# The mixer's chain: products two steps ahead, GpSimd's work reordered, and unread products on TensorE

## The chip, the cores and the metric

The kernel runs on one core of a Trainium2 chip, as one launch. The metric is device time in microseconds (us). Engines are TensorE (PE; PEld is its weight load), VectorE (DVE), ScalarE (ACT), GpSimd (POOL) and SyncE (SP, which only issues transfers here). Each engine runs its own instructions in order and waits on semaphores for the others. Numbers of lines are those of the kernel before.

## The reference, cut to what matters

The whole program is a small vision tower: an embedding, a recurrent mixer, a mixture of experts, a spiking attention, an attention block and MLPs. The change is in the mixer (`_L0_attn_ref`). With batch 4, 513 tokens, 6 heads of 64 channels and 8 states per head it computes

```
z  = s * (z - d * a * xs + d * bu)        # bu = B[t] (8) outer u[t] (64), per head
xs = xs + d * z
y[t] = C[t] . xs                          # sum over the 8 states
out = ((y + D_skip * u) * silu(gate)) @ w_out
```

one token after the other. s, d and a are numbers per token and head.

## The kernel before

The recurrence is linear, so the kernel cuts each sequence into chunks of L = 57 tokens: 9 chunks by 4 sequences make 36 steps. `mixer_responses` has computed on DVE how each lane answers (G_s, end_trans). `mixer_bc` (L1087) prepares B and C for all steps, and `mixer_chain` (L1224) walks the 36 steps, chunk by chunk with the four sequences in turn, so that a step needs the state of the step four before it. fp32 values are used in two fp16 parts, a high one and the rest ("low").

Each step n of the chain has these parts; the names in brackets are used in the text.

- POOL masks C by head: 6 copies of C side by side, each with the rows of one head, for C's high part (L1282, cbh) and for its low part (L1287, cbl). It also makes the matrix that carries the state on (L1294, [transition], for the first 32 steps), and multiplies the finished result of an earlier step with the gate (L1275, [gate]).
- PE turns u into tokens by channels (L1327, [turn], 3 fp32 transposes), carries the old state (L1355) and reads it out (L1356), both from the fifth step on ([old]), forms C times B for all heads (L1336 and L1338, [CB], 342 columns each), adds the end of chunk to the state (L1365, [send], 6 products, first 32 steps), and multiplies u with the mixing matrix (L1374, [y], 12 products of 57 columns).
- ACT rounds u to fp16 (L1312, [u high]), rounds the mixing matrix into two places (L1316, [wh], two copies), and scales u by D_skip (L1318, [D], three pieces).
- DVE takes u's rest (L1386, [u low]), multiplies CB with G_s into the mixing matrix (L1391, [matrix]), masks the new state (L1411, [state]), takes the matrix's rest (L1398, [low]; it reads two operands in SBUF), and adds D_skip times u to y (L1421, [yd]).

The order is written out by hand in each engine's block, with buffers for two steps. ACT's order is u high(n), wh(n), D(n), then u high(n+1). DVE's is u low(n+1), matrix(n+1), state(n), low(n+1), yd(n). PE's is turn(n+1), old(n), CB(n+1), send(n), y(n). POOL's is cbh(n), cbl(n), transition(n), gate(n-2).

In `mixer_bc`, PE transposes C scaled, B and C in 15 groups, ACT copies them out of PSUM as fp16 (B once, C twice, since C's high part stands in two row ranges under the low part of B), and DVE subtracts for the low parts (`low_part`). After B's low parts DVE computes the end-of-chunk matrices (L1218), ACT rounds them (L1167, L1168) and POOL subtracts (L1155), which ends the block. The halves lie in `c.xT`, a tile that is used again later and whose row DH holds ones.

`spin` (L128) issues 256-column fp16 products of ones that nobody reads; the kernel before uses it in other stages, not here. A block ends when all engines have ended theirs; `to_tokens` (L796) then multiplies by w_out.

Of the kernel before, what the change touches and what calls it, by code (L numbers as in the profile page):

```python
# [7 lines left out]
ALU = mybir.AluOpType  # L8
# [21 lines left out]
L = 57  # L30
# [96 lines left out]

def spin(c, pe, n):  # L128

    ones = c.ones[:, :].bitcast(F16)
    for _ in range(n):
        pe.matmul(c.bank[7][:, 0:256], ones[:, 0:128], ones, start=True, stop=True)  # L134

# [599 lines left out]
def mixer(c):  # L735

    with ExitStack() as ctx:
# [20 lines left out]
        half.ch = place[0][0:112, NT:2 * NT]  # L758
        half.cl = place[1][0:48, 0:NT]
        half.wh = c.sb(ctx, "B_end_high", [128, NBC * 96], F16)  # L760
# [326 lines left out]
def mixer_bc(c, ctx, raw, gs, ab, zx, acT, half):  # L1087
# [30 lines left out]
    with nc.Block() as block:  # L1118
# [24 lines left out]
        @block.gpsimd  # L1143
        def _(pool):

            pool.memset(acT[0:96].rearrange("p b s k t -> p (b s k t)"), 0.0).then_inc(zeroed, 1)  # L1146
            pool.wait_ge(zeroed, 1)
            pool.memset(half.b[32:64, :], 0.0).then_inc(zeroed, 1)
            pool.memset(half.ch[32:64, :], 0.0).then_inc(zeroed, 1)
            pool.memset(half.wh[32:64, :], 0.0).then_inc(zeroed, 1)  # L1150
            for r in (32, 64):
                pool.memset(half.wl[r:r + r, :], 0.0).then_inc(zeroed, 1)
            pool.wait_ge(zeroed, 6)
            pool.wait_ge(bwh, 2)
            pool.tensor_tensor(half.wl[0:L, :], bwf, half.wh[0:L, :], ALU.subtract).then_inc(bwl, 1)  # L1155

        @block.scalar
        def _(act):
            act.activation(bcn[0:L].rearrange("p a b c -> p (a b c)"), raw[:, :], ACT.Square).then_inc(squares, 1)
            act.wait_ge(sm, 1)  # L1160
            act.activation(sr[0:L, :], ss[0:L, :], ACT.Sqrt).then_inc(rt, 1)
            act.wait_ge(zeroed, 4)
            for n in range(len(jobs)):
# [6 lines left out]
                if kind == 0:  # L1170
                    act.copy(half.b[0:48, cols], ps[0:48]).then_inc(high, 1)
                elif kind == 1:
                    act.copy(half.ch[0:48, cols], ps[0:48]).then_inc(high, 1)
                    act.copy(half.ch[64:112, cols], ps[0:48]).then_inc(high, 1)
                else:
                    for b, ch, m, at in started(n):
                        for g in range(3):
                            rows = slice(32 * g, 32 * g + 32)
                            act.copy(acT[rows, b, ch - 1:ch - 1 + m, g, :],
                                     ps[rows, at * L:(at + m) * L].rearrange("p (a t) -> p a t", a=m)).then_inc(acd, 1)  # L1180

        @block.vector
        def _(dve):
# [19 lines left out]
            def low_part(n):  # L1203
                kind, cols, ps = job(n)
                dve.wait_ge(high, n - 4 if kind == 0 else 5 + 2 * (n - 9))
                if kind == 0:
                    dst, hi = half.b[64:112, cols], half.b[0:48, cols]
                else:
                    dst, hi = half.cl[:, cols], half.ch[0:48, cols]
                dve.tensor_tensor(dst, ps[0:48], hi, ALU.subtract).then_inc(low, 1)  # L1210
# [13 lines left out]
def mixer_chain(c, ctx, sg, vT, gs, acT, half, de, dsk, wo, wo_in):  # L1224

    nc = c.nc
    LOW = 64  # L1230
    K = LOW + L
    cbh = c.sb(ctx, "C_by_head_high", [112, 2, SH, L], F16)
    cbl = c.sb(ctx, "C_by_head_low", [112, 2, SH, L], F16)
    mask = c.sb(ctx, "head_mask", [112, SH], F16)
# [10 lines left out]
     s_done, s_ready) = map(c.sem, names)  # L1245
    skipped, padded = (c.sem(q) for q in ("Du_ready", "chain_padded"))
    N = NBC
    steps = [(ch, b, b * NC1 + ch) for ch in range(NC1) for b in range(BATCH)]
    last = N - BATCH
    with nc.Block() as block:  # L1250
# [5 lines left out]
        def _(pool):  # L1256

            for r in (32, 64):
                pool.memset(wl[r:r + r, :, :, :], 0.0).then_inc(padded, 1)
                pool.memset(cbl[r:(64, 112)[r // 64], :, :, :], 0.0).then_inc(padded, 1)  # L1260
            pool.wait_ge(padded, 4)
            pool.memset(u[32:64, :, :], 0.0).then_inc(init, 1)
# [8 lines left out]
            def gate(n):  # L1271
# [4 lines left out]
                pool.wait_ge(gated, n + 1)  # L1276

            for n, (ch, b, bc_) in enumerate(steps):
                cols = slice(bc_ * L, (bc_ + 1) * L)
                if n >= 2:  # L1280
                    pool.wait_ge(cb_done, n - 1)
                pool.tensor_tensor(cbh[:, n % 2, :, :], half.ch[:, cols].unsqueeze(1).broadcast_to((112, SH, L)),  # L1282
                                   mask[:, :].unsqueeze(2).broadcast_to((112, SH, L)), ALU.mult).then_inc(cbd_ready, 1)
                if n:
                    pool.wait_ge(cbd_ready, 2 * n)
                pool.wait_ge(cbd_ready, 2 * n + 1)
                pool.tensor_tensor(cbl[0:48, n % 2, :, :], half.cl[:, cols].unsqueeze(1).broadcast_to((48, SH, L)),  # L1287
                                   mask[0:48, :].unsqueeze(2).broadcast_to((48, SH, L)), ALU.mult
                                   ).then_inc(cbd_ready, 1)
                pool.wait_ge(cbd_ready, 2 * n + 2)  # L1290
                if n < last:
                    if n >= 2:
                        pool.wait_ge(s_done, n - 1)
                    pool.tensor_tensor(tm[:, n % 2, :].rearrange("p (h z m) -> p h z m", z=2, m=ST),  # L1294
                                       c.const("same", 96).rearrange("p (h z m) -> p h z m", z=2, m=ST),
                                       de[:, :, bc_].unsqueeze(1).unsqueeze(3).broadcast_to((96, SH, 2, ST)), ALU.mult
                                       ).then_inc(tm_ready, 1)
                    pool.wait_ge(tm_ready, n + 1)
                if n >= 2:
                    gate(n - 2)  # L1300
            for n in (N - 2, N - 1):
                gate(n)

        @block.scalar
        def _(act):
            act.wait_ge(init, 2)
            for n in range(N):
                act.wait_ge(u_t, n + 1)
# [3 lines left out]
                act.copy(u[0:L, n % 2, :], c.bank[n % 2][0:L, 0:DIN]).then_inc(u_high, 1)  # L1312
                cols = slice(steps[n][2] * L, (steps[n][2] + 1) * L)
                act.wait_ge(wt_ready, n + 1)
                for r in (0, LOW):
                    act.copy(wh[r:r + L, n % 2, :, :], wt[:, n % 2, :, :]).then_inc(wt_high, 1)  # L1316
                for k in range(3):
                    act.activation(vT[:, k, cols], vT[:, k, cols], ACT.Copy, scale=dsk[:, k:k + 1]).then_inc(skipped, 1)  # L1318

        @block.tensor  # L1320
        def _(pe):
# [8 lines left out]
            def c_times_b(n):  # L1330
                cols = slice(steps[n][2] * L, (steps[n][2] + 1) * L)
                pe.wait_ge(cbd_ready, 2 * n + 2)
                if n >= 2:
                    pe.wait_ge(wt_ready, n - 1)
                ps = c.bank[2 + n % 2][0:L, 0:SH * L]
                pe.matmul(ps, half.b[:, cols], cbh[:, n % 2, :, :].rearrange("p a b -> p (a b)"),  # L1336
                          start=True, stop=False)
                pe.matmul(ps, half.b[:, cols], cbl[:, n % 2, :, :].rearrange("p a b -> p (a b)"),  # L1338
                          start=False, stop=True).then_inc(cb_done, 1)

            turn(0)
            pe.wait_ge(padded, 4)
            c_times_b(0)
            for n, (ch, b, bc_) in enumerate(steps):
                old = state[:, b, (ch - 1) % 2, :]
                ybank, send = c.bank[4 + n % 2], c.bank[6 + n % 2][0:96, 0:2 * SP]
                if n + 1 < N:
                    turn(n + 1)
                if n >= 2:
                    pe.wait_ge(y_used, n - 1)  # L1350
                if ch:
                    pe.wait_ge(s_ready, n - BATCH + 1)
                    if n < last:
# [3 lines left out]
                              start=True, stop=False, skip_group_check=True)  # L1357
                if n + 1 < N:
                    c_times_b(n + 1)
                pe.wait_ge(u_low, n + 1)  # L1360
# [19 lines left out]
        def _(dve):  # L1380
            def prepare(n):
                ch, b, bc_ = steps[n]
                dve.wait_ge(u_high, n + 1)
                if n >= 2:
                    dve.wait_ge(y_done, n - 1)
                dve.tensor_tensor(u[LOW:LOW + L, n % 2, :], c.bank[n % 2][0:L, 0:DIN], u[0:L, n % 2, :], ALU.subtract  # L1386
                                  ).then_inc(u_low, 1)
                dve.wait_ge(cb_done, n + 1)
                if n >= 2:
# [10 lines left out]

            dve.wait_ge(padded, 4)
            prepare(0)
            low_part(0)
            for n, (ch, b, bc_) in enumerate(steps):
                if n + 1 < N:
                    prepare(n + 1)
                if n < last:
# [11 lines left out]
                if n >= 2:  # L1419
                    dve.wait_ge(gated, n - 1)  # L1420
                dve.tensor_tensor(yd[:, n % 2, :, :], c.bank[4 + n % 2][:, 0:3 * L].rearrange("p (k t) -> p k t", k=3),  # L1421
                                  vT[:, :, bc_ * L:(bc_ + 1) * L], ALU.add).then_inc(y_used, 1)


# [1712 lines left out]
```

## Time and profile before

| | us |
|---|---|
| median of 3 runs | 1843.28 (1840.26 to 1844.48) |
| profiled execution | 1847.83, its span 1846.0 |
| PE, DVE, ACT, POOL busy | 1513.2, 1306.5, 1053.0, 411.4 |
| chain's block, from its first turn to its last gate | 527.3 to 654.5 |

PE's busy time counts matmuls as pipelined work with modelled ends, so that a full 20 of 20 us need not be full speed. PEclk is the share of TensorE's 2.4 GHz that was granted: 1.00 is 2.4 GHz and 0.50 is 1.2 GHz. The page's 40 slices, 46 us each, show it by stage:

```profile
PEclk9999997688555588987999756999598889999898
```

Slices 11 to 14 of them (from 461 us to 646 us) are the scan's end, `mixer_bc` and the chain. An x behind a row is the count of instructions. "Idle before, releaser" in brackets is the time in which the engine stood still before the first of them, and what ended it.

### The profile page before, as it was taken

The page shows a single profiled execution, that of the slowest core. Times are in us where ns is not written, and L with a number is a line of the kernel's source. Part 1 is how long each engine was busy: PE and PEld are TensorE (multiplying, and loading weights), DVE is VectorE, ACT ScalarE, POOL GpSimd, SP SyncE. Part 2 cuts the span into 40 slices and gives each one's busy share as a digit, 9 for nine tenths or more (in the row PEclk, how much of TensorE's full clock was granted, in tenths as well). Part 3 has the DMA queues.
Part 4 walks back from the last instruction along what each step waited for, and adds up shares of the span by engine and source line. Part 5 has one row for each costly group of instructions (what it writes and reads, how often), then busy time and mean ns, then how long its engine had stood idle before and what let it go on. Part 6 is the DMA issues. An engine that isn't in the chain of part 4 may idle for free. (4 is left out here: it accounts for less than half of the span.)

```text
span 1846.0 us, 36517 instructions
## 1 busy us (share of the span) xinstructions
PE 1513.2 (82%) x14190; PEld 1135.7 (62%) x14190; DVE 1306.5 (71%) x2831; ACT 1053.0 (57%) x1872; POOL 411.4 (22%) x428
## 2 busy tenths in 40 slices
PE   5898995877349987899999854998198899999795
PEld 5888985776326675764444544888086554446474
DVE  5988895489646655837999375887365469995666
ACT  6988994433356616444998423665100548896455
POOL 0000000000357711036980013665000320000100
PEclk9999997688555588987999756999598889999898
DMA  5120001000000010002540092121200000000101
GB/s 138 27 65 23 14 2 48 1 4 1 1 7 1 1 33 1 14 1 104 180 131 2 1 271 66 56 62 50 73 1 5 9 2 2 2 2 2 33 1 35
DMA packets 52725, 67.96 MB, mean 37 GB/s; under 512 B 11511, under 2 KB 41465, under 8 KB 52554
## 3 DMA queue, kind: packets, MB, share of 16 engines
q1 hardware_dynamic: 46586, 50.74, 9.0%
q0 software_dynamic: 3840, 9.18, 1.7%
q10 hardware_dynamic: 2128, 5.71, 1.2%
q8 instruction: 114, 1.87, 0.4%
q14 instruction: 57, 0.47, 0.1%
HBM read 46.97 MB, written 18.65 MB: 36 GB/s over the span
## 5 line engine op out<-in xcount | busy, mean ns | idle before, releaser
L2007 DVE TENSOR_REDUCE att_max<-banks 104x1 f32<-104x512 f32 (+1 forms) x480 | 295.9, 682 | 9.7 <-PE banks L1921 5.7
L2042 ACT ACTIVATE att_p<-banks 104x514 f32<-104x514 f32 (+1 forms) x480 | 262.3, 600 | 33.3 <-PE banks L1966 22.6
L339 PE MATMUL banks<-tok_wT,feature_halves 128*128 128x192 f16 x2592 | 229.5, 249 | 22.9 <-DVE feature_halves L365 11.8
L339 PEld LDWEIGHTS banks<-tok_wT,feature_halves 128*128 128x128 f16 x2592 | 217.4, 99 | 31.8 <-DVE feature_halves L365 17.5
L1982 PE MATMUL banks<-att_p,att_v 104*32 104x257 f32 (+1 forms) x1920 | 159.8, 405 | 0.9 <-ACT att_p L2042 0.3
L1966 PE MATMUL banks<-att_q,att_kT 64*104 64x257 f16 (+1 forms) x960 | 155.9, 304 | 2.9 <-ACT att_p L2042 2.5
L1921 PE MATMUL banks<-att_kT,att_q 64*104 64x512 f16 (+1 forms) x480 | 126.3, 424 | 4.9 <-DVE att_max L2007 2.1
L365 DVE TENSOR_TENSOR feature_halves<-features,feature_halves 128x2048 f16<-128x2048 f32 x54 | 123.4, 2285 | 6.1 <-ACT feature_halves L462 6.1
L1966 PEld LDWEIGHTS banks<-att_q,att_kT 64*104 64x104 f16 (+1 forms) x960 | 61.8, 123 | 107.0 <-ACT att_p L2042 80.2
L1146 POOL MEMSET C_start_apart<- 96x5472 f32 x1 | 4.7, 4658 | 476.0 <-POOLq L972 476.0
L462 ACT CAST feature_halves<-features 128x2048 f16<-128x2048 f32 x54 | 102.2, 1893 | 10.8 <-PE banks L339 10.0
L134 PE MATMUL banks<-ones 128*128 128x256 f16 x450 | 59.9, 302 | 56.3 <-PEq L113 27.3
L134 PEld LDWEIGHTS banks<-ones 128*128 128x128 f16 x450 | 48.1, 108 | 67.9 <-issue 53.7
L2761 ACT COPY slot_xT<-banks 128x512 f16<-128x512 f16 x40 | 23.4, 586 | 93.4 <-PE banks L2711 93.4
L2740 PE MATMUL banks<-expert_w,slot_hidden_halves 128*128 128x192 f16 x720 | 65.8, 246 | 12.1 <-DVE slot_hidden_halves L2809 12.1
L2724 PE MATMUL banks<-slot_xT,expert_w 128*128 128x128 f16 x1200 | 75.7, 223 | 0.0
L1819 DVE TENSOR_TENSOR att_qkv_parts<-banks,att_qkv_parts 104x192 f16<-104x192 f32 (+1 forms) x80 | 25.0, 354 | 70.7 <-ACT att_qkv_parts L1799 70.7
L354 DVE SCALAR_TENSOR_TENSOR angle_rest<-raw_T,freq,turns 128x1024 f32<-128x1024 f32 x54 | 69.0, 1278 | 6.2 <-ACT turns L244 5.7
L2699 POOL DMA_INDIRECT expert_out<-slot_y,slot_goes x40 | 61.4, 1536 | 49.1 <-DMA expert_out<-slot_y,slot_goes 38.2
L1758 PE MATMUL banks<-att_qkv_w,xT 96*104 96x384 f32 (+3 forms) x160 | 66.7, 543 | 6.7 <-POOL att_qkv_parts L1734 4.5
L2724 PEld LDWEIGHTS banks<-slot_xT,expert_w 128*128 128x128 f16 x1200 | 72.0, 100 | 0.0
L1921 PEld LDWEIGHTS banks<-att_kT,att_q 64*104 64x104 f16 (+1 forms) x480 | 51.9, 126 | 31.3 <-DVE att_max L2007 19.2
(463 smaller groups left out, 3532.6 us busy)
## 6 DMA issues: line engine op xcount, KB each, us to landing
expert_w_in<-in_L_ffn_w_dram SPq DMA_DIRECT2D x16, 576.0 KB, 4.5
expert_w_halves<-expert_w_halves SPq DMA_DIRECT2D x32, 288.0 KB, 2.5
tok_w<-in_L_tok_W_dram ACTq DMA_DIRECT2D x4, 1152.0 KB, 7.3
expert_w2s<-expert_w_halves SPq DMA_DIRECT2D x1, 4608.0 KB
expert_y<-expert_out SPq DMA_DIRECT2D x6, 513.0 KB
expert_w1s<-expert_w_halves SPq DMA_DIRECT2D x2, 1536.0 KB
raw<-in_x_dram SPq DMA_DIRECT2D x2, 1152.0 KB, 5.7
expert_w1s<-expert_w_halves SPq DMA_DIRECT2D x3, 768.0 KB
```

The source lines that it names most:

```text
L134: pe.matmul(c.bank[7][:, 0:256], ones[:, 0:128], ones, start=True, stop=True)
L339: ins = pe.matmul(c.bank[t // 2][:, (t % 2) * D:(t % 2 + 1) * D], fh[:, s, q, z, t * 128:(t + 1) * 128], wT[:, y, k, 6 * q + wf, :], start ...
L354: own.did(dve.scalar_tensor_tensor(fr[:, n % 2, :], rT[:, k, hf * HALF:(hf + 1) * HALF], freq_col(k, f), fm[:, n % 2, :], ALU.mult, ALU.su ...
L365: dve.tensor_tensor(fh[:, s, :, 1, :], feat[:, s, :, :], fh[:, s, :, 0, :], ALU.subtract).then_inc(flow, 1)
L462: act.copy(fh[:, s, :, 0, :], feat[:, s, :, :]).then_inc(fhigh, 1)
L1758: ins = pe.matmul(c.bank[n % 2][0:m, 0:2 * D], c.xT[0:r, o, at:at + m], w[0:r, o, 0:2 * D], start=(o == 0), stop=(o == 1))
L1921: pe.matmul(bank_of(("s", n))[0:qn, 0:KEYS], q2[r, 2 * j + gi, b * T + q0:b * T + q0 + qn], kT[r, 2 * j + gi, b * T:b * T + KEYS], start=T ...
L1966: pe.matmul(c.pair[2 + n % 2][0:kn, 512 * e:512 * e + HALF], kT[r, 2 * j + gi, b * T + k0:b * T + k0 + kn], q2[r, 2 * j + gi, b * T + STAR ...
L1982: ins = pe.matmul(acc[32 * hh:32 * hh + 32, 0:HALF], v[0:kn, b, k, h, :], p[0:kn, (n + hh // 2) % 4, hh % 2, :], start=(k == 0), stop=(k = ...
L2007: dve.reduce_max(mx[0:qn, n // NS % 2, 2 * gi + e, k:k + 1], bank_of(unit)[0:qn, 0:KEYS], X).then_inc(maxed, 1)
L2042: act.activation(p[0:kn, n % 4, :, :], c.pair[2 + n % 2][0:kn, :].rearrange("p (e q) -> p e q", e=2)[:, :, 0:HALF], ACT.Exp, scale=scale). ...
L2724: ins = pe.matmul(ps, ws[:, s, at:at + 128], xt[:, s, b, :], start=(k == 0), stop=(k == len(TERMS) - 1))
```

## The change

- CB needs one masked tile: C's high and low parts stand under each other (rows 0 to 47 and 64 to 111) and B in two tiles, its high part in both row ranges and its low part over zeros. So B is copied twice in `mixer_bc` and C once, POOL masks once per step (cbd, as many columns and rows as cbh), and two more memsets clear B's second tile.
- That tile covers the row of ones in `c.xT`; POOL writes it again behind the last gate (1 x 1026 fp32).
- PE's turn, CB and with it DVE's matrix run two steps ahead, not one. DVE's order is then u low(n+1), state(n), low(n+1), yd(n), matrix(n+2).
- POOL's order is cbd(n), gate(n-3), transition(n-1).
- PE issues 36 unread products between turn(1) and the first CB, and 3 before each CB, into the bank that CB then overwrites.

```diff
-def spin(c, pe, n):
+def spin(c, pe, n, bank=7):
-        pe.matmul(c.bank[7][:, 0:256], ones[:, 0:128], ones, start=True, stop=True)
+        pe.matmul(c.bank[bank][:, 0:256], ones[:, 0:128], ones, start=True, stop=True)
...
-        half.cl = place[1][0:48, 0:NT]
+        half.bl = place[1][0:112, 0:NT]
...
+            pool.memset(half.bl[32:64, :], 0.0).then_inc(zeroed, 1)
             pool.memset(half.wh[32:64, :], 0.0).then_inc(zeroed, 1)
+            pool.memset(half.bl[64:112, :], 0.0).then_inc(zeroed, 1)
-            pool.wait_ge(zeroed, 6)
+            pool.wait_ge(zeroed, 8)
...
-            act.wait_ge(zeroed, 4)
+            act.wait_ge(zeroed, 5)
...
                 if kind == 0:
                     act.copy(half.b[0:48, cols], ps[0:48]).then_inc(high, 1)
+                    act.copy(half.b[64:112, cols], ps[0:48]).then_inc(high, 1)
                 elif kind == 1:
                     act.copy(half.ch[0:48, cols], ps[0:48]).then_inc(high, 1)
-                    act.copy(half.ch[64:112, cols], ps[0:48]).then_inc(high, 1)
...
-                dve.wait_ge(high, n - 4 if kind == 0 else 5 + 2 * (n - 9))
+                dve.wait_ge(high, 2 * (n - 4) if kind == 0 else n + 1)
                 if kind == 0:
-                    dst, hi = half.b[64:112, cols], half.b[0:48, cols]
+                    dst, hi = half.bl[0:48, cols], half.b[0:48, cols]
                 else:
-                    dst, hi = half.cl[:, cols], half.ch[0:48, cols]
+                    dst, hi = half.ch[64:112, cols], half.ch[0:48, cols]
                 dve.tensor_tensor(dst, ps[0:48], hi, ALU.subtract).then_inc(low, 1)
...
-    cbh = c.sb(ctx, "C_by_head_high", [112, 2, SH, L], F16)
-    cbl = c.sb(ctx, "C_by_head_low", [112, 2, SH, L], F16)
+    cbd = c.sb(ctx, "C_by_head", [112, 2, SH, L], F16)
...
             for r in (32, 64):
                 pool.memset(wl[r:r + r, :, :, :], 0.0).then_inc(padded, 1)
-                pool.memset(cbl[r:(64, 112)[r // 64], :, :, :], 0.0).then_inc(padded, 1)
-            pool.wait_ge(padded, 4)
+            pool.wait_ge(padded, 2)
...
+            def transition(n):
+                bc_ = steps[n][2]
+                if n >= 2:
+                    pool.wait_ge(s_done, n - 1)
+                pool.tensor_tensor(tm[:, n % 2, :].rearrange("p (h z m) -> p h z m", z=2, m=ST),
+                                   c.const("same", 96).rearrange("p (h z m) -> p h z m", z=2, m=ST),
+                                   de[:, :, bc_].unsqueeze(1).unsqueeze(3).broadcast_to((96, SH, 2, ST)), ALU.mult
+                                   ).then_inc(tm_ready, 1)
+                pool.wait_ge(tm_ready, n + 1)
             for n, (ch, b, bc_) in enumerate(steps):
                 cols = slice(bc_ * L, (bc_ + 1) * L)
                 if n >= 2:
                     pool.wait_ge(cb_done, n - 1)
-                pool.tensor_tensor(cbh[:, n % 2, :, :], half.ch[:, cols].unsqueeze(1).broadcast_to((112, SH, L)),
+                pool.tensor_tensor(cbd[:, n % 2, :, :], half.ch[:, cols].unsqueeze(1).broadcast_to((112, SH, L)),
                                    mask[:, :].unsqueeze(2).broadcast_to((112, SH, L)), ALU.mult).then_inc(cbd_ready, 1)
-                if n:
-                    pool.wait_ge(cbd_ready, 2 * n)
-                pool.wait_ge(cbd_ready, 2 * n + 1)
-                pool.tensor_tensor(cbl[0:48, n % 2, :, :], half.cl[:, cols].unsqueeze(1).broadcast_to((48, SH, L)),
-                                   mask[0:48, :].unsqueeze(2).broadcast_to((48, SH, L)), ALU.mult
-                                   ).then_inc(cbd_ready, 1)
-                pool.wait_ge(cbd_ready, 2 * n + 2)
...
-                if n >= 2:
-                    gate(n - 2)
-            for n in (N - 2, N - 1):
+                pool.wait_ge(cbd_ready, n + 1)
+                if n >= 3:
+                    gate(n - 3)
+                if 1 <= n <= last:
+                    transition(n - 1)
+            for n in (N - 3, N - 2, N - 1):
                 gate(n)
+            pool.wait_ge(cb_done, N)
+            pool.memset(c.xT[DH:DH + 1, 1, 0:NT // 2], 1.0).then_inc(ones_row, 1)
...
-            act.wait_ge(init, 2)
-            for n in range(N):
+            def highs(n):
                 act.wait_ge(u_t, n + 1)
                 if n >= 2:
                     act.wait_ge(y_done, n - 1)
                     act.wait_ge(s_done, min(n - 1, last))
                 act.copy(u[0:L, n % 2, :], c.bank[n % 2][0:L, 0:DIN]).then_inc(u_high, 1)
-                cols = slice(steps[n][2] * L, (steps[n][2] + 1) * L)
                 act.wait_ge(wt_ready, n + 1)
                 for r in (0, LOW):
                     act.copy(wh[r:r + L, n % 2, :, :], wt[:, n % 2, :, :]).then_inc(wt_high, 1)
+            act.wait_ge(init, 2)
+            for n in range(N):
+                highs(n)
+                cols = slice(steps[n][2] * L, (steps[n][2] + 1) * L)
                 for k in range(3):
                     act.activation(vT[:, k, cols], vT[:, k, cols], ACT.Copy, scale=dsk[:, k:k + 1]).then_inc(skipped, 1)
...
             def c_times_b(n):
                 cols = slice(steps[n][2] * L, (steps[n][2] + 1) * L)
-                pe.wait_ge(cbd_ready, 2 * n + 2)
+                pe.wait_ge(cbd_ready, n + 1)
                 if n >= 2:
                     pe.wait_ge(wt_ready, n - 1)
                 ps = c.bank[2 + n % 2][0:L, 0:SH * L]
-                pe.matmul(ps, half.b[:, cols], cbh[:, n % 2, :, :].rearrange("p a b -> p (a b)"),
+                spin(c, pe, 3, 2 + n % 2)
+                pe.matmul(ps, half.b[:, cols], cbd[:, n % 2, :, :].rearrange("p a b -> p (a b)"),
                           start=True, stop=False)
-                pe.matmul(ps, half.b[:, cols], cbl[:, n % 2, :, :].rearrange("p a b -> p (a b)"),
+                pe.matmul(ps, half.bl[:, cols], cbd[:, n % 2, :, :].rearrange("p a b -> p (a b)"),
                           start=False, stop=True).then_inc(cb_done, 1)
 
             turn(0)
-            pe.wait_ge(padded, 4)
+            turn(1)
+            spin(c, pe, 36, 4)
+            pe.wait_ge(padded, 2)
             c_times_b(0)
+            c_times_b(1)
             for n, (ch, b, bc_) in enumerate(steps):
                 old = state[:, b, (ch - 1) % 2, :]
                 ybank, send = c.bank[4 + n % 2], c.bank[6 + n % 2][0:96, 0:2 * SP]
-                if n + 1 < N:
-                    turn(n + 1)
+                if n + 2 < N:
+                    turn(n + 2)
                 if n >= 2:
                     pe.wait_ge(y_used, n - 1)
                 if ch:
@@ -1355,8 +1364,8 @@
                         pe.matmul(send, tm[:, n % 2, :], old, start=True, stop=False, skip_group_check=True)
                     pe.matmul(ybank[:, 0:3 * L], old, acT[0:96, b, ch - 1, :, :].rearrange("p k t -> p (k t)"),
                               start=True, stop=False, skip_group_check=True)
-                if n + 1 < N:
-                    c_times_b(n + 1)
+                if n + 2 < N:
+                    c_times_b(n + 2)
...
-            def prepare(n):
-                ch, b, bc_ = steps[n]
+            def u_low_part(n):
                 dve.wait_ge(u_high, n + 1)
                 if n >= 2:
                     dve.wait_ge(y_done, n - 1)
                 dve.tensor_tensor(u[LOW:LOW + L, n % 2, :], c.bank[n % 2][0:L, 0:DIN], u[0:L, n % 2, :], ALU.subtract
                                   ).then_inc(u_low, 1)
+            def matrix(n):
+                ch, b, bc_ = steps[n]
...
-            dve.wait_ge(padded, 4)
-            prepare(0)
+            dve.wait_ge(padded, 2)
+            matrix(0)
+            u_low_part(0)
+            matrix(1)
             low_part(0)
             for n, (ch, b, bc_) in enumerate(steps):
                 if n + 1 < N:
-                    prepare(n + 1)
+                    u_low_part(n + 1)
...
+                if n + 2 < N:
+                    matrix(n + 2)
```

## Rows read from the trace of the kernel before

**Rows 1.** Windows of the chain: PE, PEld, DVE, ACT, POOL busy (x), then PEclk

```profile
560.00:593.25 33.25, 33.25 (x271) 21.54 (x270) 20.79 (x51) 21.21 (x62) 25.48 (x40) 0.50 0.01 2
643.00:653.00 10.00, 6.80 (x54) 4.20 (x56) 5.46 (x13) 6.39 (x19) 4.57 (x7) 0.50 0.00 0
```

**Rows 2.** Instructions on the mixing matrix: ns min/median/max, first and last start

```profile
L1391 DVE TENSOR_TENSOR mix_matrix<-banks,G_s x36: 505/506/507, 534.4 to 650.8; 57x342 f32<-57x342 f32 x36
L1398 DVE TENSOR_TENSOR mix_matrix_low<-mix_matrix,mix_matrix_high x36: 506/508/706, 535.9 to 652.3; 57x342 f16<-57x342 f32 x36
```

**Rows 3.** Timeline of one step, DVE and ACT: start, us

```profile
587.59 0.51 DVE L1391 TENSOR_TENSOR mix_matrix<-banks,G_s 57x342 f32<-57x342 f32 x1
588.13 0.98 ACT L1316 CAST mix_matrix_high<-mix_matrix 57x342 f16<-57x342 f32 x2 [1.16 <-DVE mix_matrix L1391]
589.13 0.81 ACT L1318 ACTIVATE u_T<-u_T,D_skip 128x57 f32<-128x57 f32 x3
589.14 0.62 DVE L1398 TENSOR_TENSOR mix_matrix_low<-mix_matrix,mix_matrix_high 57x342 f16<-57x342 f32 x1 [0.84 <-ACT mix_matrix_high L1316]
589.69 0.32 DVE L1421 TENSOR_TENSOR y_plus_Du<-banks,u_T 128x171 f32<-128x171 f32 x1
589.85 0.45 ACT L1312 CAST u_halves<-banks 57x384 f16<-57x384 f32 x1
590.34 0.55 DVE L1386 TENSOR_TENSOR u_halves<-banks,u_halves 57x384 f16<-57x384 f32 x1 [0.33 <-ACT u_halves L1312]
```

**Rows 4.** Timeline of the same step, PE

```profile
587.46 0.89 PE L1327 MATMUL banks<-consts,u_T 128*57 128x128 f32 x3
588.15 0.63 PE L1355 MATMUL banks<-xT,transition 96*96 96x128 f32 x2
589.28 0.49 PE L1336 MATMUL banks<-C_by_head_high,xT 112*57 112x342 f16 x1
589.98 0.30 PE L1365 MATMUL banks<-u_halves,B_end_high 121*32 121x128 f16 x3
590.77 0.89 PE L1327 MATMUL banks<-consts,u_T 128*57 128x128 f32 x3
```

**Rows 5.** Timeline of the same step, POOL

```profile
589.05 0.35 POOL L1294 TENSOR_TENSOR transition<-consts,end_trans 96x96 f32<-96x96 f32 x1
590.15 0.51 POOL L1275 TENSOR_TENSOR gate_silu<-y_plus_Du,gate_silu 128x171 f32<-128x171 f32 x1 [0.76 <-PE banks L1338]
590.75 0.76 POOL L1282 TENSOR_TENSOR C_by_head_high<-xT,head_mask 112x342 f16<-112x342 f16 x1
```

**Rows 6.** Timeline of a step in which POOL's mask and DVE's low part overlap

```profile
598.59 0.75 POOL L1287 TENSOR_TENSOR C_by_head_low<-xT,head_mask 48x342 f16<-48x342 f16 x1
599.12 0.59 DVE L1398 TENSOR_TENSOR mix_matrix_low<-mix_matrix,mix_matrix_high 57x342 f16<-57x342 f32 x1 [0.84 <-ACT mix_matrix_high L1316]
```

**Rows 7.** Windows of unread products (first two) and of a looser stage, to PEclk

```profile
318.00:320.00 2.00, 2.00 (x12) 1.42 (x10) 0.50 0.42 35
324.00:326.00 2.00, 2.00 (x21) 1.79 (x20) 1.00 0.04 8
688.00:692.00 4.00, 4.00 (x26) 2.31 (x24) 2.98 (x10) 2.54 (x3) 1.15 (x1) 1.00 0.01 2
```

**Rows 8.** Timeline of the chain's start and its end

```profile
527.30 0.86 PE L1327 MATMUL banks<-consts,u_T 128*57 128x128 f32 x3 [17.79 <-PEq L1118]
533.60 0.46 PE L1336 MATMUL banks<-C_by_head_high,xT 112*57 112x342 f16 x1 [5.44 <-POOL C_by_head_low L1287]
654.01 0.53 POOL L1275 TENSOR_TENSOR gate_silu<-y_plus_Du,gate_silu 128x171 f32<-128x171 f32 x1 [0.30 <-DVE y_plus_Du L1421]
```

**Rows 9.** Timeline of `mixer_bc`: a memset, copies of B and C, DVE's product

```profile
481.62 1.80 POOL L1148 MEMSET xT<- 32x2052 f16 x1
506.94 2.08 ACT L1171 CAST xT<-banks 48x456 f16<-48x456 f32 x5
510.08 1.95 DVE L1218 TENSOR_TENSOR bc_raw<-bc_normed,xT 57x1728 f32<-57x1728 f32 x1
511.70 0.53 ACT L1174 CAST xT<-banks 48x456 f16<-48x456 f32 x1
512.25 0.53 ACT L1173 CAST xT<-banks 48x456 f16<-48x456 f32 x1
```

More of the change, by code:

```diff
@@ L1245, in mixer_chain @@
      s_done, s_ready) = map(c.sem, names)
-    skipped, padded = (c.sem(q) for q in ("Du_ready", "chain_padded"))
+    skipped, padded, ones_row = (c.sem(q) for q in ("Du_ready", "chain_padded", "ones_row_again"))
     N = NBC
@@ L1281, in _ @@
                     pool.wait_ge(cb_done, n - 1)
-                pool.tensor_tensor(cbh[:, n % 2, :, :], half.ch[:, cols].unsqueeze(1).broadcast_to((112, SH, L)),
+                pool.tensor_tensor(cbd[:, n % 2, :, :], half.ch[:, cols].unsqueeze(1).broadcast_to((112, SH, L)),
                                    mask[:, :].unsqueeze(2).broadcast_to((112, SH, L)), ALU.mult).then_inc(cbd_ready, 1)
-                if n:
-                    pool.wait_ge(cbd_ready, 2 * n)
-                pool.wait_ge(cbd_ready, 2 * n + 1)
-                pool.tensor_tensor(cbl[0:48, n % 2, :, :], half.cl[:, cols].unsqueeze(1).broadcast_to((48, SH, L)),
-                                   mask[0:48, :].unsqueeze(2).broadcast_to((48, SH, L)), ALU.mult
-                                   ).then_inc(cbd_ready, 1)
-                pool.wait_ge(cbd_ready, 2 * n + 2)
-                if n < last:
-                    if n >= 2:
[L1293 to L1299, printed above, removed]
-                    gate(n - 2)
-            for n in (N - 2, N - 1):
+                pool.wait_ge(cbd_ready, n + 1)
[4 more added lines that the diff above has]
+            for n in (N - 3, N - 2, N - 1):
                 gate(n)
+            pool.wait_ge(cb_done, N)
+            pool.memset(c.xT[DH:DH + 1, 1, 0:NT // 2], 1.0).then_inc(ones_row, 1)
         @block.scalar
         def _(act):
-            act.wait_ge(init, 2)
-            for n in range(N):
+            def highs(n):
                 act.wait_ge(u_t, n + 1)
```

## The prediction

> **What bounds the kernel now.** I read the page first: 1513.2 of 1846.0 us are PE's, but slices 11 to 14 of its PEclk row stand at 5 tenths, where others stand at 9. So I went to that stage. The windows of the chain [rows 1] show two things. In mid-chain PE is never idle (33.25 of 33.25 us) and yet granted 0.50, that is 1.2 GHz. In the last steps, where the send products are gone, PE is busy for 6.80 of 10.00 us, so something else holds the pace there. The list of instructions on the mixing matrix names it: matrix (L1391) starts at 534.4 first and at 650.8 last, 35 intervals of 3.326 us [rows 2], and this pace is the same in the middle and at the end.
>
> The timeline of one step gives the loop [rows 3]. It is wh to D 1.00 (588.13 to 589.13), D to u high 0.72, u high to u low 0.49, u low to the next matrix 0.57 (to 590.91, one interval behind 587.59), matrix to wh 0.54: 3.32 us. It closes because D stands ahead of u high on ACT, and matrix(n+1) behind u low(n+1) on DVE. PE has the same pace by itself: one turn to the next is 3.31 us (587.46 to 590.77) with no part waiting [rows 4]. So there are two bounds within 0.02 us of each other, and a change that lifts only one brings nothing. This one goes at both.
>
> **The loop of ACT and DVE.** With matrix two steps ahead, wh no longer waits for the u low that follows D. The new order closes as matrix to wh 0.54, wh to low 1.01, low to yd 0.43 (0.55 in the row, less the 0.12 by which that low exceeds the median of 0.508 in [rows 2]), yd to matrix 0.24 to 0.32 (its length is 0.32, and neighbours on DVE overlap by up to 0.08): 2.25 us [rows 3]. u low and state (0.55 and about 0.3) fit between matrix and low. ACT alone needs 1.00 + 0.72 + 0.45 = 2.17.
>
> **POOL against low.** A mask is taken away (0.75, [rows 6]), so POOL works 0.51 + 0.35 + 0.76 with gaps, some 1.85 us a step. But the new order puts cbd right behind transition, and these behind the gate that yd released. By rows: yd's end to gate 0.14, gate to the next operation 0.60, transition to the next 0.45 (0.35 and a gap of 0.1), cbd 0.76 [rows 3, 5]. cbd then stands at 1.2 to 1.95 us behind the matrix's start, and low wants to start at 1.55. Where POOL's mask overlapped low before, low ended 0.37 us behind the mask's end (599.71 against 599.34) and took 0.59 instead of 0.51 [rows 6]. So low's end is set by POOL: 0.14 + 0.60 + 0.45 + 0.76 + 0.37, then 0.07 back to yd's start and 0.32 for yd: 2.57 us. That is the value I take for a step; 2.25 is the lower end.
>
> The Trainium skill has this as a rule ("SBUF — State Buffer", Who interferes with whom): a DVE operation with two inputs in SBUF and a GpSimd operation that reads SBUF exclude each other, and the second one waits until the first is through. The trace agrees in kind. Taken to the letter low would begin only at the mask's end and end 0.51 behind it, not 0.37; by that a step is 2.71 us, and 33 x 0.14 = 4.6 us of the gain below would go.
>
> **PE.** At 1.2 GHz a step costs 3.31 and the 3 unread products of 256 columns 0.64 (a column per cycle), 3.95 us. At 2.4 GHz the streaming halves. Of the 3.31 about 2.7 are columns (turn 0.69, the two state products 1.0, CB 0.57, send and y about 0.45 between their starts and the next [rows 4]); so a step is (2.7 + 0.64) / 2 + 0.6 = 2.27 us, and if nothing of send, y and the gaps halves, 2.6. Either fits under 2.57 or barely so. Everything therefore hangs on the granted clock. Unread products brought it from 0.50 (at 318 to 320 us) to 1.00 by 324, where twice as many fit [rows 7]. It then stayed at 1.00 in a stage in which PE had 26 small products in 4 us [rows 7], which is looser than this chain will be. I take 1.00 for the chain, with the start and the last four steps in doubt.
>
> **The chain's sum.** Before, matrix(0) to matrix(35) is 116.4 us [rows 2]. After: matrix(0) to matrix(2) is 0.54 + 1.00 + 0.72 + 0.45 + 1.01 + 0.43 + 0.3 = 4.45 [rows 3], then 33 x 2.57 = 84.8; together 89.3, **27.1 less**. From matrix(35) on both kernels do the same.
>
> **The chain's start: 1.7 more.** The first turn starts at 527.3 and CB(0) at 533.6, held by POOL's memsets and masks [rows 8]. Those get shorter (two memsets and a mask go), but now PE has two turns (1.4) and 36 unread products: 7.7 us if all run at 1.2 GHz, 5.8 if half do. I take 6.5, so CB(0) comes at 535.2, and its own 3 unread products add 0.1 net.
>
> **The block ahead: 2.2 more.** Copies of C in pairs follow each other in 0.55 (511.70 to 512.25); B's five single ones took 2.08 together [rows 9]. Five B copies more end B's low parts 2.4 us later if paired copies go at 0.55 and about 1.3 if at 0.42; DVE's end matrices (510.08), ACT's rounding and POOL's subtraction follow in a row to the end of the block, so it all shifts. I take 2.2. The copies of C that go fall into the wait for DVE and give nothing. The two memsets (1.80 each by [rows 9]) run on POOL while ACT and DVE have the norm to do; POOL had been idle behind them until 520 us. If that cover were gone they would cost 3.6.
>
> **The chain's end: 1.0 more.** The row of ones, 1026 columns at 0.88 ns (1.80 us for 2052, [rows 9]), is 0.9 and a gap, behind the last gate (654.0, [rows 8]), and nobody can start the next block before it.
>
> **Sum.** 27.1 - 1.7 - 2.2 - 1.0 = 22.2 us. The profiled execution of 1847.83 (span 1846.0) would become 1825.6; against the median, 4.55 lower, it is 1843.3 - 22.2 = **1821 us**.
>
> **The rivals.** (B) *No collision*: POOL's cbd comes later or low slips in ahead, and a step is 2.25 to 2.35. For it: POOL has some 0.7 us free per step. Against it: cbd waits for nothing but a CB that is long done. It gives 33 x 0.27 = 9 us more, 1812 to 1814.
>
> (C) *PE is the bound at 2.4 GHz too*: waits for u low, the mask and the 18 small products add to 2.27, and the step is 2.9. For it: in [rows 4] no part of PE's step overlaps another. It costs 33 x 0.33 = 11, 1832.
>
> (D) *The clock falls in the chain, slower than before*: the 36 unread products raise it, but the first steps, without old state to read and with a pipeline that is filling, leave PE waiting, it goes back to 0.50, and the chain does not lift it by itself. For it: the chain before never did in 116 us without a pause [rows 1]. Against it: 3 unread products more per step and [rows 7]. Then a step is 3.95, with 2.9 in the first four and 3.2 in the last four, 131 us for 116.4, and with 3.4 at the start (7.7 for all 36), 2.2 and 1.0 it is 21 us more: 1865. It decides from about 16 of the 36 steps at 0.50, since each costs 1.38 and 22 are to be lost.
>
> (E) *The change does not unhook the loop*: u high(n+2) waits for y(n), so if PE's y comes late ACT is held as before, a step stays near 3.3, and the three costs remain: 1848. For it is only that ACT needs 2.17 of 2.57.
>
> **How the numbers follow.** Forecast 0.55 (own range 1815 to 1827), B 0.17, C 0.12, D 0.11, E 0.05. The range reaches from B to C: 1811 to 1834; D and E and a few edges are left out, 0.2 together. A measurement of this kernel tells about 0.2% (3.7 us) from no change. Faster by more than that: forecast, B and C and a part of the partly cold cases, 0.85; within it 0.04; slower 0.11.
>
> **What would show it.** Right: PEclk near 1.0 from about 534 us to the chain's end; matrix starts 2.5 to 2.65 us apart; low at 0.75 to 0.85 us with cbd beside it; POOL's subtraction in the block ahead ending some 2 us later; a memset of 0.9 last on POOL. Low at 0.51 and 2.3 apart would be B. PE without idle time before y and DVE waiting for PE would be C. PEclk of 0.5 in the chain would be D, and then the sign is wrong. What I can't size is the clock in the stages behind, whose rises will fall at other moments; the three runs before spread over 4.2 us.

## The result, and the profile after

The changed kernel takes 1814.17 us (1807.55 to 1817.52), the kernel before 1843.83 in the same comparison: ratio 0.9839, interval 0.9808 to 0.9869, so 24 to 35 us less. The forecast was 1821 us in a range of 1811 to 1834.

The windows of the chain in the changed kernel (columns as in [rows 1]) show the clock at 1.00 and PE no longer busy all the time:

```profile
560.00:580.00 20.00, 18.59 (x240) 11.98 (x238) 18.37 (x41) 16.68 (x48) 12.93 (x24) 1.00 0.01 2
580.00:600.00 20.00, 18.59 (x240) 11.88 (x239) 18.37 (x41) 16.69 (x48) 12.70 (x25) 1.00 0.01 2
```

The instructions on the mixing matrix, against [rows 2] (the lines have moved: matrix is L1402, low is L1409):

```profile
L1402 DVE TENSOR_TENSOR mix_matrix<-banks,G_s x36: 492/494/506, 538.3 to 625.3; 57x342 f32<-57x342 f32 x36
L1409 DVE TENSOR_TENSOR mix_matrix_low<-mix_matrix,mix_matrix_high x36: 506/823/883, 539.8 to 626.8; 57x342 f16<-57x342 f32 x36
```

35 intervals now take 87.0 us, 2.53 us in mid-chain and 2.22 in the last three. low has gone from a median of 508 to one of 823 ns. The timeline of one step (POOL's lines: L1277 gate, L1284 transition, L1294 cbd) tells why, against [rows 3, 5, 6]:

```profile
580.36 0.32 DVE L1434 TENSOR_TENSOR y_plus_Du<-banks,u_T 128x171 f32<-128x171 f32 x1
580.61 0.49 DVE L1402 TENSOR_TENSOR mix_matrix<-banks,G_s 57x342 f32<-57x342 f32 x1
580.83 0.51 POOL L1277 TENSOR_TENSOR gate_silu<-y_plus_Du,gate_silu 128x171 f32<-128x171 f32 x1 [0.76 <-DVE y_plus_Du L1434]
581.13 0.98 ACT L1316 CAST mix_matrix_high<-mix_matrix 57x342 f16<-57x342 f32 x2 [0.37 <-DVE mix_matrix L1402]
581.41 0.35 POOL L1284 TENSOR_TENSOR transition<-consts,end_trans 96x96 f32<-96x96 f32 x1
581.84 0.76 POOL L1294 TENSOR_TENSOR C_by_head<-xT,head_mask 112x342 f16<-112x342 f16 x1
582.14 0.82 DVE L1409 TENSOR_TENSOR mix_matrix_low<-mix_matrix,mix_matrix_high 57x342 f16<-57x342 f32 x1
582.88 0.32 DVE L1434 TENSOR_TENSOR y_plus_Du<-banks,u_T 128x171 f32<-128x171 f32 x1
```

yd releases gate, transition and cbd follow with gaps of under 0.1 us, cbd ends at 582.60, low ends 0.36 us behind it (582.96) though it could start at 582.14, and yd follows: 2.52 us from yd to yd.

Start and end of the chain, against [rows 8, 9]:

```profile
530.27 1.50 PE L1332 MATMUL banks<-consts,u_T 128*57 128x128 f32 x6 [19.23 <-PEq L1118]
531.57 6.17 PE L134 MATMUL banks<-ones 128*128 128x256 f16 x39
628.50 0.53 POOL L1277 TENSOR_TENSOR gate_silu<-y_plus_Du,gate_silu 128x171 f32<-128x171 f32 x1 [0.30 <-DVE y_plus_Du L1434]
629.09 0.95 POOL L1304 MEMSET xT<- 1x1026 f32 x1
```

In intervals between first starts, which leaves out where the stages ahead happened to be:

| interval, us | before | after | change | forecast |
|---|---|---|---|---|
| norm's product on DVE to the chain's first turn | 38.39 | 40.73 | +2.3 | +2.2 |
| first turn to matrix(0) | 7.08 | 7.98 | +0.9 | +1.7 |
| matrix(0) to matrix(35) | 116.38 | 87.01 | -29.4 | -27.1 |
| matrix(35) to the last gate's end | 3.77 | 3.76 | 0.0 | 0 |
| last gate's end to to_tokens | 0.80 | 1.37 | +0.6 | +1.0 |
| sum | | | -25.6 | -22.2 |

The clock is at 1.00 from 535.1 to 627.3 us, so from before matrix(0) to just ahead of the last y products. The row from the first turn to matrix(0) is one execution's: five more runs below have the same 36 products there, and take 7.22 to 8.02 us for it, +0.1 to +0.9.

The two spans differ by 33.5 us, so 7.9 lie in stages that the change doesn't touch; more on these stands at the end of the experiments.

### The profile page after: what moved, and what is told of

It is laid out like the page before. It is cut to its first block and busy times, and to the rows that moved or that the text cites. A ratio compares the mean times of both kernels' runs of the same rounds, so it can differ in the third digit from the quotient of the medians.

```text
span 1812.5 us, 36735 instructions
## 1 busy us (share of the span) xinstructions
PE 1481.0 (82%) x14334; PEld 1115.6 (62%) x14334; DVE 1311.4 (72%) x2831; ACT 1052.1 (58%) x1872; POOL 383.6 (21%) x393
## 5 line engine op out<-in xcount | busy, mean ns | idle before, releaser
L134 PE MATMUL banks<-ones 128*128 128x256 f16 x594 | 82.1, 296 | 56.7 <-PEq L113 26.6
L134 PEld LDWEIGHTS banks<-ones 128*128 128x128 f16 x594 | 59.9, 106 | 73.8 <-issue 54.7
L2699 POOL DMA_INDIRECT slot_x<-token_rows,slot_comes x40 | 55.7, 1393 | 74.2 <-POOLq L2400 62.5
```

The source lines that it names most:

```text
L134: pe.matmul(c.bank[bank][:, 0:256], ones[:, 0:128], ones, start=True, stop=True)
```

## The experiments

**The collision alone.** In the changed kernel POOL's last two parts of a round change places:

```diff
-                if n >= 3:
-                    gate(n - 3)
                 if 1 <= n <= last:
                     transition(n - 1)
+                if n >= 3:
+                    gate(n - 3)
```

> The changed kernel, but POOL's order is cbd(n), transition(n-1), gate(n-3), so that cbd follows the gate directly and transition comes behind it. Theory (the step of 2.53 us is a loop over POOL: yd, gate, transition, cbd, and low blocked until cbd is through): cbd ends about 1.55 us behind the matrix's start, when low wants to start, low goes back from 0.83 to about 0.51 us, matrix starts come 2.2 to 2.3 us apart, and the kernel gains about 8 us on the changed one: ratio to before about 0.979. Rival 1 (the step is PE's own work at 2.4 GHz): 2.53 us stays, no gain. Rival 2 (low is long by itself in the new order, for another reason than cbd beside it): low stays at 0.83.

Measured: ratio 0.9796 (0.978 to 0.9813), median 1805.32 us. Its instructions on the matrix and its timeline:

```profile
L1402 DVE TENSOR_TENSOR mix_matrix<-banks,G_s x36: 493/496/506, 535.9 to 613.7; 57x342 f32<-57x342 f32 x36
L1409 DVE TENSOR_TENSOR mix_matrix_low<-mix_matrix,mix_matrix_high x36: 495/506/879, 537.5 to 615.3; 57x342 f16<-57x342 f32 x36
```

```profile
580.64 0.98 ACT L1316 CAST mix_matrix_high<-mix_matrix 57x342 f16<-57x342 f32 x2
580.91 0.76 POOL L1294 TENSOR_TENSOR C_by_head<-xT,head_mask 112x342 f16<-112x342 f16 x1
581.64 0.81 ACT L1323 ACTIVATE u_T<-u_T,D_skip 128x57 f32<-128x57 f32 x3
581.69 0.50 DVE L1409 TENSOR_TENSOR mix_matrix_low<-mix_matrix,mix_matrix_high 57x342 f16<-57x342 f32 x1
581.75 0.65 POOL L1284 TENSOR_TENSOR transition<-consts,end_trans 96x96 f32<-96x96 f32 x1
582.36 0.46 ACT L1313 CAST u_halves<-banks 57x384 f16<-57x384 f32 x1
```

cbd now ends at 581.67, just ahead of low; low is back at 0.50, and it is transition, second to come, that waits for low (0.65, not 0.35), where it costs nothing. From the third interval on steps are 2.21 to 2.25 us and the chain is 77.8 us, 9.2 less. So the 2.53 us were the loop over POOL: the same products of PE and the same low now fit in less. DVE's u low, which reads one operand in PSUM, has cbd beside it here and takes 0.55 us as before. At 2.25 ACT has no pause left (580.64 to 581.64 to 582.36 to the next wh at 582.89), and PE is busy for 20.00 of 20 us (window of 580 to 600 us); which of the two bounds this step no run here separates.

**One bound lifted, the clock.** The kernel before with the unread products only:

```diff
             turn(0)
+            spin(c, pe, 36, 4)
...
                 ps = c.bank[2 + n % 2][0:L, 0:SH * L]
+                spin(c, pe, 3, 2 + n % 2)
```

> The kernel before, with nothing changed but the unread products: 36 behind the first turn and 3 ahead of each CB. Theory (two bounds of 3.3 us, one of PE at 1.2 GHz and one of the loop over ACT and DVE): the clock rises to 1.00 and stays, PE then has idle time in each step, and matrix starts stay 3.32 us apart; the kernel is 1 to 3 us slower than before for its later start. Rival (the clock was the gain): matrix starts come closer, 2.5 to 2.8 us apart, and the kernel gains 15 us or more.

Measured: ratio 1.0002 (0.9987 to 1.0017). Two windows of its chain, and behind them its matrix instructions:

```profile
542.00:552.00 10.00, 8.21 (x61) 4.50 (x61) 6.01 (x15) 6.37 (x18) 7.04 (x13) 0.50 0.01 2
580.00:600.00 20.00, 14.49 (x180) 9.12 (x180) 12.39 (x30) 12.78 (x37) 15.11 (x25) 1.00 0.01 2
```

```profile
L1393 DVE TENSOR_TENSOR mix_matrix<-banks,G_s x36: 504/506/507, 535.0 to 652.0; 57x342 f32<-57x342 f32 x36
```

PE falls from a full window [rows 1] to 14.49 of 20 us at the upper level, and matrix stays 3.32 us apart: the clock alone gives nothing. "Rises to 1.00 and stays" missed: the clock fell again from 541.8 to 552.1 us and then rose by itself. In that stretch two intervals took 3.48 and 3.87 us, which is the 0.6 us that this chain is longer than the one before; all others took 3.32 or 3.33.

**The other bound lifted, the order.** The changed kernel without any unread product:

```diff
-                spin(c, pe, 3, 2 + n % 2)
...
-            spin(c, pe, 36, 4)
```

> The changed kernel without any unread product, so the new order of the work alone. Theory (PE at 1.2 GHz has a bound of 3.31 us a step of its own): PEclk stays 0.50 through the chain, matrix starts 3.31 us apart, DVE and ACT wait for PE; the chain starts 4 us earlier than with the 36 products; the time is that of the kernel before within 4 us. Rival (the new order gives most of the gain): 2.6 to 3.0 us a step at 0.50 and a gain of 10 us or more.

Measured: ratio 0.9935 (0.991 to 0.9959), 1832.73 us. Its windows, and behind them its matrix instructions:

```profile
540.00:560.00 20.00, 19.97 (x173) 12.67 (x171) 14.72 (x35) 15.21 (x43) 11.35 (x21) 0.50 0.01 2
560.00:580.00 20.00, 20.00 (x164) 13.01 (x164) 11.55 (x30) 13.55 (x37) 9.84 (x19) 0.50 0.00 1
```

```profile
L1400 DVE TENSOR_TENSOR mix_matrix<-banks,G_s x36: 493/496/506, 534.5 to 642.6; 57x342 f32<-57x342 f32 x36
```

3.31 us a step at 0.50 in mid-chain, as the theory has it. "Within 4 us of before" missed: it is about 11 us faster. In the trace the chain is 8.3 us shorter. Intervals three to six, where PE has little or no old state to read yet, take 2.5 us even at 1.2 GHz, the loop over POOL as at 2.4 GHz; the last two, without send, take 2.2 us. The clock rose at 639.9 us, within the first of these two, but in no_step_spins below the first of them also takes 2.24 us, and there it lies before the rise. Together the two halves give 29.4 us in the chain, where one alone gives -0.6 and the other 8.3.

**The 3 products per step.** Taken away, the 36 left:

```diff
-                spin(c, pe, 3, 2 + n % 2)
```

> The changed kernel without the 3 unread products per step; the 36 at the start stay. Theory A (the chain's own products hold the clock once it is up, as a looser stage did at 688 us): PEclk stays 1.00, steps of 2.53 us, same time as the changed kernel within 3 us. Theory B (the 3 per step are needed): the clock falls in the first steps, which have no old state to read, or later, and from there the steps are 3.3 us long at 0.50: 15 to 25 us slower than the changed kernel.

Measured: ratio 0.9994 (0.9971 to 1.0017), 1843.73 us. Theory B:

```profile
533.00:539.00 6.00, 4.77 (x50) 3.19 (x47) 2.57 (x5) 2.35 (x7) 2.71 (x5) 0.99 0.00 0
540.00:560.00 20.00, 19.68 (x175) 11.74 (x175) 14.80 (x36) 15.60 (x46) 11.36 (x21) 0.50 0.01 2
560.00:580.00 20.00, 20.00 (x164) 13.09 (x164) 11.71 (x32) 13.55 (x37) 9.73 (x18) 0.50 0.00 1
```

The clock fell at 539.9 us, in the second interval, and stayed down for 102 of the chain's 108 us (to 642.3). The time is 29 us over the changed kernel, more than the 15 to 25 expected; the chain accounts for 21 of them, and the rest is open. So I asked which steps need them:

```diff
-                spin(c, pe, 3, 2 + n % 2)
+                if n < 8:
+                    spin(c, pe, 3, 2 + n % 2)
```

> The changed kernel with the 3 unread products only ahead of the first eight CBs, none ahead of the other 28. Without any the clock fell within the first steps, which have no old state to read. Theory A (only those steps are too loose; from the fifth step on the chain's own products hold 1.00): PEclk 1.00 to the chain's end, steps of 2.53 us, time of the changed kernel within 3 us. Theory B (all steps need them): the clock falls soon after the eighth CB and stays at 0.50, 3.31 us a step for some 28 steps: 20 us more than the changed kernel in the chain.

Measured: ratio 0.9839 (0.981 to 0.9869), that of the changed kernel. Theory A, with less PE work than in the changed kernel and the clock still up to the chain's end:

```profile
580.00:600.00 20.00, 15.60 (x216) 10.35 (x216) 18.37 (x41) 16.70 (x49) 12.79 (x24) 1.00 0.01 2
600.00:620.00 20.00, 15.35 (x209) 10.04 (x207) 18.08 (x40) 16.99 (x50) 12.51 (x23) 1.00 0.00 1
```

**The 36 products.**

```diff
-            spin(c, pe, 36, 4)
```

> The changed kernel without the 36 unread products at the start; the 3 per step stay. Theory A (at 1.2 GHz a step with 3 unread products leaves PE no pause, 3.95 us long, and that lifts the clock after some steps): PEclk goes to 1.00 within the first 10 steps, the chain starts 5 us earlier and loses up to that in its slow steps: within 5 us of the changed kernel. Theory B (it never rises, as it never did in the kernel before): 3.95 us a step in mid-chain, 40 us or more slower than the changed kernel, and slower than before by some 15.

Measured: ratio 0.9898 (0.9873 to 0.9923), 1821.77 us, from 1810.3 to 1827.28: 7.6 us over the changed kernel, where "within 5 us" was expected. In the profiled execution (the fastest) the clock rose within the first two steps:

```profile
530.00:538.00 8.00, 5.25 (x21) 2.47 (x19) 2.27 (x4) 2.48 (x7) 6.30 (x13) 0.51 0.13 37
538.00:540.00 2.00, 2.00 (x29) 1.21 (x28) 1.80 (x6) 1.95 (x7) 0.08 (x1) 1.00 0.00 0
```

Two others had a mean granted clock of 0.874 and 0.876 over the whole execution, where this one had 0.887. They fit a rise that comes later in the chain, but that is not shown: there is no trace of them, and b_copies_later below, whose start has the 36 products, spreads over 13 us with clocks from 0.877 to 0.891. What is shown is that the kernel with the 36 products is faster by time, though they cost 1.4 to 2.2 us at the start (first turn to matrix(0) 5.86 without them, 7.22 to 8.02 with).

**The two costs, and a start with fewer products.** Three kernels, each on top of the one before, start from the new order of POOL. The first writes the row of ones ahead of the last two gates:

```diff
-            for n in (N - 3, N - 2, N - 1):
-                gate(n)
+            gate(N - 3)
             pool.wait_ge(cb_done, N)
             pool.memset(c.xT[DH:DH + 1, 1, 0:NT // 2], 1.0).then_inc(ones_row, 1)
+            pool.wait_ge(ones_row, 1)
+            for n in (N - 2, N - 1):
+                gate(n)
```

> mask_behind_gate, with the row of ones written ahead of the last two gates instead of behind the last. Theory (the memset adds its 0.95 us and a gap to the chain's end because POOL's last gate already sets it): the last gate to the first product of to_tokens becomes 0.8 us as in the kernel before, about 1 us shorter. Rival (the next block waits for something else): no change in that interval.

Last gate to to_tokens: 0.53 us against 1.36 in mask_behind_gate, 0.8 less. There is one execution, 1804.33 us, so its time shows nothing. The second moves B's second copies (only the lines that matter):

```diff
                 if kind == 0:
                     act.copy(half.b[0:48, cols], ps[0:48]).then_inc(high, 1)
-                    act.copy(half.b[64:112, cols], ps[0:48]).then_inc(high, 1)
                 elif kind == 1:
                     act.copy(half.ch[0:48, cols], ps[0:48]).then_inc(high, 1)
+                    bcols = job(n - 5)[1]
+                    act.wait_ge(high, n - 9)
+                    act.copy(half.b[64:112, bcols], half.b[0:48, bcols]).then_inc(b_again, 1)
...
-                dve.wait_ge(high, 2 * (n - 4) if kind == 0 else n + 1)
+                dve.wait_ge(high, n - 4)
```

> ones_row_earlier, and in the block ahead of the chain the second copy of B's high part is made from the first one in SBUF, next to the copies of C, where ACT waits anyway. Theory (the five extra copies ahead of B's low parts delay DVE's end matrices and all behind them): the end of the norm to the chain's first turn becomes as long as in the kernel before, 2.4 us shorter. Rival (the block's end is set by ACT's total work or by PE's transposes): it stays.

Norm to first turn: 38.26 us, as before the change (38.39), against 40.71. Ratio 0.9787 (0.9747 to 0.9826): too wide to show 2.4 us by time. The third uses PE's idle time in the block ahead:

```diff
+            pe.wait_ge(low, 5)
+            pe.wait_ge(bwh, 1)
+            spin(c, pe, 56)
...
-            spin(c, pe, 36, 4)
+            spin(c, pe, 20, 4)
```

> b_copies_later, and 56 unread products at the end of PE's work in the block ahead, behind B's first rounding, with 20 instead of 36 between turn(1) and the first CB. PE had stood idle there. Theory: the clock is at 1.00 when the chain starts, turn and 20 products take 2.9 us instead of 7.8, so the first matrix comes 3 to 4 us earlier or waits for POOL's first mask; steps stay at 2.22 us; 1799 to 1802 us in all. Rival (the pause between the blocks lets the clock fall again): the first steps run at 0.50 and nothing is gained.

Measured: ratio 0.9773 (0.9747 to 0.9799), 1802.64 us (1799.25 to 1804.03). First turn to matrix(0) is 5.53 us against 7.58, 2.0 less and not 3 to 4. The rival was partly right: the clock was up from 521.0 us, before the block's end, and down again at 527.8 us, behind a pause of 2.0 us in PE's work and half a microsecond into the chain (first turn at 527.3),

```profile
522.00:525.00 3.00, 3.00 (x30) 2.70 (x28) 0.00 (x0) 0.00 (x0) 3.00 (x1) 1.00 0.00 0
528.00:530.00 2.00, 2.00 (x11) 1.42 (x10) 0.00 (x0) 0.00 (x0) 1.94 (x3) 0.50 0.54 150
530.00:532.20 2.20, 2.20 (x16) 1.59 (x13) 0.00 (x0) 0.47 (x1) 1.91 (x6) 0.72 0.02 5
```

so some 0.5 us of the gain are the two turns, which still ran mostly at the upper clock (the unread products begin 0.80 us behind the first turn, where it was 1.30), and the rest is that there were 16 products fewer to wait for. This version has the lowest median, 40 us under the kernel before. Its interval overlaps that of mask_behind_gate, so against that one it is shown by the intervals of the trace and not by time.

**What the stages behind do.** The code behind the chain is the same in all eleven profiled executions, yet its time is not. The stage from the experts' second product to the spiking block took 158.5 to 164.6 us, and from there to the end 539.6 to 551.7. From the first product of to_tokens to the end it was 1190.7 us before and 1182.1 after, 8.6 less; the stages ahead of the norm's product took 0.6 more, which leaves the 7.9. This is not plain scatter: that stretch took 1190.1 to 1192.4 us in the four kernels whose chain is 108 us or longer, 1181.0 to 1182.1 in the three at 87 us, and 1184.7 to 1189.0 in the four at 78. The trace shows the clock rising and falling at other moments in each. So the change may move the clock in these stages too, but with one trace of each kernel that is not shown. The chain's 25.6 us alone lie inside the interval of the timed runs.

## Why the prediction was right

The mechanism held in each of its steps, and the time is 7 us under the forecast but in the range. Of these 7, about 3 come from the terms below and 4 from stages that the forecast put at nothing, which was luck in so far as they stayed small.

- *Two bounds within 0.02 us*: held. Lifting the clock alone left 3.32 us a step, lifting the order alone 3.31 in mid-chain. What I left out is that PE at 1.2 GHz is a bound only where it has its full step, so "a change that lifts only one brings nothing" was too strong: the order alone gave 8.3 us of chain.
- *2.57 us over POOL*: measured 2.53; gate, transition and mask came at 0.15, 0.58 and 0.43 us where I had 0.14, 0.60 and 0.45. *low ends 0.37 behind the mask's end*: 0.36. I carried 2.57 to the last step; the last three have no transition and take 2.22, which with the 0.04 makes the chain's 2.3 us more. By the letter of the rule in the Trainium skill ("SBUF — State Buffer", Who interferes with whom) low would have begun at the mask's end and the step been 2.71. The trace agrees in kind, that the second one waits, but low's recorded duration began 0.46 us before the mask was through and it ended 0.36 behind it; alone it takes 0.51.
- *PE at 2.27 a step at 2.4 GHz*: it has idle time at 2.53 (18.59 of 20 us, some 2.35 a step), so rival C is out, and mask_behind_gate does the same products in steps of 2.21 to 2.25. The upper figure of 2.6 should read 2.5 by its own terms (half of 0.69, 1.0, 0.57 and 0.64, and 1.05 for the rest); nothing hangs on it.
- *The clock*: it stayed at 1.00. Rival D's mechanism is real, though it did not strike here: without the 3 products per step the clock fell in the first steps, as D has it, and in the kernel before it fell at 541.8 us even with them. Rival B was what happens if cbd comes earlier, not later, and was worth 9.2 us, as I had put it.
- *Start +1.7*: mis-sized, +0.9 here and +0.1 to +0.9 over six executions of this start. The 36 products took 5.8 us, my lower bound, not 6.5, and mostly less in those where the clock rose sooner. *Block ahead +2.2*: 2.3. *End +1.0*: the memset took 0.95, but to_tokens then began 0.36 us behind it, where it had begun 0.80 behind the last gate, so 0.6 net.
- What is open of the time is 4 us between the chain's 25.6 and the medians' 29.7. It is within the interval; whether it is scatter or an effect of the change on the stages behind is open.

## What to carry to other kernels

Work out every engine's own pace and every loop over two engines before touching one of them; here two stood within 0.02 us and each half alone was worth nothing or, in the chain, a bit over a quarter. When an order changes, lay POOL's SBUF reads beside DVE's operations with two SBUF operands, and put the long POOL operation where DVE has one operand in PSUM. Where TensorE's clock matters, look for the few loose steps at the start: unread products there were enough here (ahead of the stage and in its first eight steps; fewer steps were not tried), with the rest of the chain at 15.60 of 20 us busy.

## What the runs showed that I had not expected

In mid-chain the chain's own products hold the upper clock but do not lift it. With 28 steps without an unread product the clock stayed at 1.00 (PE 15.60 of 20 us busy), and the same steps in the same order stayed at 0.50 (PE 20.00 of 20) after the first ones had let it fall. It rose only at 642.3 us, where the steps have no send any more (639.9 in no_spins). In the kernel before, with 3 unread products per step, it rose at 552.1 us although PE was busy for only 8.21 of the 10 us ahead of that. So the busy share of the profile alone does not tell whether the clock will rise; which of PE's work counts no run here shows. A fall early in a stage thus cost 102 us at the lower clock, and 21 us of time in the chain.
